# Delta stage on 32x32 tiles in token order, chunks of 64 tokens, filter products moved into the scan

## The reference

```python
q, k, v = short_conv(x @ Wq), short_conv(x @ Wk), short_conv(x @ Wv)   # 4 heads of 32
beta = sigmoid(x @ Wb); q, k = l2norm(q), l2norm(k); v = v * beta; kb = k * beta
A = -tril(kb @ k.T, -1)                       # per chunk of 32 tokens
T = solve_triangular(eye - A, eye, lower=True)
u = T @ v; w = T @ kb
def step(S, (qi, ki, ui, wi)):                # scan over the chunks
    attn = tril(qi @ ki.T)
    u_i = ui - wi @ S
    o_i = qi @ S + attn @ u_i
    return S + ki.T @ u_i, o_i
branches = [fir(v, fir_s), fir(v, fir_l), delta_o, v]   # filters of 3 and 31 taps
o = sum(gate(x, branches) * branches) ... @ Wo
```

## Time and profile before

| what | us |
|---|---|
| median of 3 runs | 594.73 |
| lowest, highest | 591.89, 598.05 |
| profiled execution, its time | 600.54 |
| its span in the trace | 598.8 |
| PE / PEld busy | 439.1 / 333.1 |
| DVE / ACT / POOL busy | 322.3 / 225.3 / 142.4 |

### The profile page before, as it was taken

The page is one execution under the profiler, slowest core; times in us unless marked ns, Lnnn a source line. Parts: engine busy times, 40 slices in busy tenths (PEclk is TensorE's granted clock), DMA queues, the critical chain, the costliest instruction groups (busy, mean ns, idle before and its releaser), DMA issues. The chain is left out here.

```text
span 598.8 us, 12845 instructions
## 1 busy us (share of the span) xinstructions
PE 439.1 (73%) x5009; PEld 333.1 (56%) x5010; DVE 322.3 (54%) x819; ACT 225.3 (38%) x453; POOL 142.4 (24%) x154
## 2 busy tenths in 40 slices
PE   0782699926976588899999999995999344029990
PEld 0682399913545467677875655563355344029890
DVE  4540355436965697776444654327368884216533
ACT  1232045514565278884231000017457222005550
POOL 4336025520006980000000000002023200733441
PEclk9999889966897679999679965558799655559996
DMA  9963301130000000000000000005400036140015
GB/s 174 261 199 88 101 15 37 35 89 1 0 1 0 4 4 4 5 4 3 1 2 1 2 0 1 0 1 123 106 1 1 0 120 197 44 128 24 32 35 155
DMA packets 32710, 29.93 MB, mean 50 GB/s; under 512 B 6800, under 2 KB 25776, under 8 KB 32656
## 3 DMA queue, kind: packets, MB, share of 16 engines
q1 hardware_dynamic: 23760, 20.96, 12.6%
q10 hardware_dynamic: 6400, 3.08, 3.4%
q0 software_dynamic: 2496, 5.13, 2.6%
HBM read 16.54 MB, written 9.21 MB: 43 GB/s over the span
## 5 line engine op out<-in xcount | busy, mean ns | idle before, releaser
L303 ACT ACTIVATE hT<-bank,b1s 128x128 f32<-128x128 f32 x184 | 52.4, 370 | 90.8 <-PE bank L260 90.6
L206 POOL DMA_INDIRECT ysort<-Y,row x46 | 44.8, 974 | 78.7 <-DVE Y L382 72.6
L260 PE MATMUL bank<-xT,w1s 128*128 (+1 forms) x368 | 51.5, 285 | 2.8 <-DVE xT L405 2.8
L276 PE MATMUL bank<-W,hT 128*128 x368 | 50.8, 281 | 3.6 <-ACT hT L303 3.1
L260 PEld LDWEIGHTS bank<-xT,w1s 128*128 128x128 f32 x368 | 47.0, 200 | 4.1 <-DVE xT L405 3.6
L1386 POOL TENSOR_TENSOR m_DSQ<-DEL 128x512 f32<-128x512 f32 x4 | 4.1, 1041 | 187.8 <-POOLq L767 185.1
L276 PEld LDWEIGHTS bank<-W,hT 128*128 128x128 f32 x368 | 45.2, 193 | 6.0 <-issue 5.8
L1056 DVE TENSOR_TENSOR d_BD<-bank,quarter 128x2048 f32<-128x2048 f32 x16 | 36.6, 2289 | 14.2 <-PE bank L760 14.2
L199 POOL DMA_INDIRECT xsort<-xr,pos x32 | 31.4, 981 | 48.4 <-DVE pos L361 39.3
L901 PE MATMUL bank<-XN,K 32*128 32x128 f32 x128 | 40.2, 403 | 1.6 <-DVE XN L1092 1.6
L966 ACT ACTIVATE d_BD<-d_TP 32x512 f32<-32x512 f32 x64 | 40.6, 634 | 0.9
(11 more groups left out here) (297 smaller groups left out, 939.4 us busy)
## 6 DMA issues: line engine op xcount, KB each, us to landing
W<-in_L_ffn_w SPq DMA_DIRECT2D x2, 2048.0 KB, 13.4
xsort<-pad ACTq DMA_DIRECT2D x2, 1483.5 KB, 23.1
xs<-xsort SPq DMA_DIRECT2D x10, 258.0 KB, 4.3
G<-ysort SPq DMA_DIRECT2D x8, 256.0 KB, 3.8
b2bc<-in_L_ffn_b SPq DMA_DIRECT2D x2, 512.0 KB, 20.3
m_pairs<-FS SPq DMA_DIRECT2D x4, 256.0 KB, 5.0
m_pairs<-firT SPq DMA_DIRECT2D x4, 256.0 KB, 4.9
m_pairs<-VP SPq DMA_DIRECT2D x4, 256.0 KB, 5.1
```

The costliest lines, as they stand in the source:

```text
L206: gp.indirect_dma_start(ysort, bass.IndirectOffsetOnAxis(row[:, t:t + 1], 0), Y[:, t, :], None).then_inc(y_stored, 16)
L260: mm = pe.matmul(pH[s % 2][:, j * P:(j + 1) * P], w1s[:, s, j * P:(j + 1) * P], xT[:, bass.ds(t, 1), :], start=True, stop=True)
L276: mm = pe.matmul(pY[s % 2][:, 0:D], hT[:, s % 2, j, :], W2[:, bass.ds(e, 1), j, :], start=(j == 0), stop=(j == FC - 1))
L303: act.activation(hT[:, s % 2, j, :], pH[s % 2][:, j * P:(j + 1) * P], ACT.Gelu, bias=b1s[:, s, j:j + 1]).then_inc(h_ready, 1)
```

## The change

Only `attn_delta` changes in what it computes, and in `attn_consts` the masks that it needs.

- The blocks of A and T are kept as `[P, head, tile, 32]` with the chunk on the partitions. Nothing is block-diagonal any more. A takes 256 products of 32x32x32, and 128 more (`a10`) give the off-diagonal blocks of the 64-token chunks.
- The inverse takes 16 steps, four levels by four heads. A step is `first` and `second`, each 64 products of 32x32x32; DVE masks 128x512 (instead of 128x2048), adds 128x512 and transposes on DVE. The PE transposes and ACT's copies are gone.
- `off_first` and `off_second` (32 products each, once per head) make the off-diagonal blocks of the 64-token inverse `T64`, with 16 copies by ACT, 8 by POOL and 8 by DVE.
- Scores: 128 products of 32 rows by 64 by 64. T @ v and T @ kb: 128 products each, on 64-row tiles, with results already in the layout that the scan reads.
- Scan: 16 steps of 64 tokens. `intra` moves into it (four matmuls per step and sequence). The 512 matmuls of `long_fir` move from the inverse into the first eight steps, 64 a step; `turn_fl` moves to steps 10 to 15, three transposes a step.
- `make_masks` gets three more selects of 128x128 on POOL in place of one, and `finish` five more reductions on DVE.

```diff
+    C, W = 32, 64
...
+    STEPS = NL * NH
+    STEPS_S = L // W
...
+    CH = 2 * P // STEPS_S
...
+AT = sb("AT", [P, NH, NT, C])
+TN = sb("TN", [P, NH, NT, C])
+TT = sb("TT", [P, NH, NT, C])
+PM = sb("PM", [P, 2, NT, C])
+OX = sb("OX", [P, NH, NT, C])
+T64 = sb("T64", [P, NH, NT, W])
...
+    for n in range(NT):
+        for c in range(CT):
+            for h in range(NH):
+                mm = pe.matmul(banks[h][quad(c), n * C:(n + 1) * C], KT[quad(h), tokens(n, c)], KBT[quad(h), tokens(n, c)],
+                               start=True, stop=True)
+    mm.then_inc(at_psum, 1)
+    for n in range(NT):
+        for p in range(HT):
+            for h in range(NH):
+                mm = pe.matmul(banks[4 + h][quad(2 * p), n * C:(n + 1) * C], KT[quad(h), tokens(n, 2 * p)],
+                               KBT[quad(h), tokens(n, 2 * p + 1)], start=True, stop=True)
+    mm.then_inc(a10_psum, 1)
+    pe.wait_ge(a10_ready, NH)
+    def first(s):
+        h = s % NH
+        pe.wait_ge(t_ready, s + 1)
+        if s >= 2:
+            pe.wait_ge(p1_ready, s - 1)
+        for n in range(NT):
+            for c in range(CT):
+                mm = pe.matmul(banks[4 + s % 2][quad(c), n * C:(n + 1) * C], AT[quad(c), h, n, :], TN[quad(c), h, n, :],
+                               start=True, stop=True)
+        mm.then_inc(p1_psum, 1)
+    def second(s):
+        h = s % NH
+        pe.wait_ge(p1_ready, s + 1)
+        if s >= 2:
+            pe.wait_ge(t_ready, NH + s - 1)
+        for n in range(NT):
+            for c in range(CT):
+                mm = pe.matmul(banks[6 + s % 2][quad(c), n * C:(n + 1) * C], PM[quad(c), s % 2, n, :], TT[quad(c), h, n, :],
+                               start=True, stop=True)
+        mm.then_inc(dt_psum, 1)
+    for s in range(STEPS):
+        first(s)
+        if s > 0:
+            second(s - 1)
+    second(STEPS - 1)
+    def scores(r):
+        if r == 0:
+            pe.wait_ge(at_ready, NH)
+        else:
+            pe.wait_ge(m_ready, NH)
+        for n in range(r * TH, (r + 1) * TH):
+            for p in range(HT):
+                for h in range(NH):
+                    mm = pe.matmul(banks[h][wide(p), n % TH * W:(n % TH + 1) * W], KT[quad(h), chunk(n, p)],
+                                   QT[quad(h), chunk(n, p)], start=True, stop=True)
+        mm.then_inc(m_psum, 1)
+    def off_first(h):
+        pe.wait_ge(t_ready, STEPS + h + 1)
+        if h >= 2:
+            pe.wait_ge(x_ready, h - 1)
+        for n in range(NT):
+            for p in range(HT):
+                mm = pe.matmul(banks[4 + h % 2][quad(2 * p + 1), n * C:(n + 1) * C], OX[quad(2 * p), h, n, :],
+                               TN[quad(2 * p), h, n, :], start=True, stop=True)
+        mm.then_inc(x_psum, 1)
+    def off_second(h):
+        pe.wait_ge(x_ready, h + 1)
+        if h < 2:
+            pe.wait_ge(t_ready, NH + STEPS)
+        else:
+            pe.wait_ge(t10_ready, h - 1)
+        for n in range(NT):
+            for p in range(HT):
+                mm = pe.matmul(banks[6 + h % 2][quad(2 * p), n * C:(n + 1) * C], OX[quad(2 * p + 1), h, n, :],
+                               TT[quad(2 * p + 1), h, n, :], start=True, stop=True)
+        mm.then_inc(t10_psum, 1)
+    off_first(0)
+    off_first(1)
+    scores(0)
+    off_second(0)
+    off_first(2)
+    off_second(1)
+    off_first(3)
+    off_second(2)
+    scores(1)
+    off_second(3)
+    pe.wait_ge(t10_ready, NH)
+    pe.wait_ge(even_ready, HT * NH)
+    pe.wait_ge(odd_ready, NH)
+    pe.wait_ge(m_ready, 2 * NH)
     for g in range(NG):
...
+        for n in range(g * TB, (g + 1) * TB):
+            for h in range(NH):
+                for p in range(HT):
+                    o = n % TB * P + h * DK
+                    mm = pe.matmul(banks[g][wide(p), o:o + DK], T64[wide(p), h, n, :], VB[wide(p), n, quad(h)], start=True, stop=True)
+        mm.then_inc(u0_psum, 1)
+        for n in range(g * TB, (g + 1) * TB):
+            for h in range(NH):
+                for p in range(HT):
+                    mm = pe.matmul(banks[4 + 2 * p + n // TH][quad(h), n % TH * W:(n % TH + 1) * W], KB[wide(p), n, quad(h)],
+                                   T64[wide(p), h, n, :], start=True, stop=True)
+        mm.then_inc(wt_psum, 1)
     pe.wait_ge(u0_ready, NG)
...
     pe.wait_ge(wt_ready, NG)
...
+    def intra(b, n):
+        p, tile = n % HT, b * TH + n // HT
+        for h in range(NH):
+            mm = pe.matmul(o_place(tile)[wide(p), quad(h)], M[h][wide(p), tile, :], U[wide(p), tile, quad(h)], start=False, stop=True,
+                           skip_group_check=True)
+        if p == HT - 1 and tile % TB == TB - 1:
+            mm.then_inc(o_psum, 1)
+    def long_fir(i):
+        j = i * CH // 2 // CB
+        if i * CH // 2 % CB == 0 and j >= 2:
+            pe.wait_ge(fir_taken, j - 1)
+        for c in range(i * CH // 2, (i + 1) * CH // 2):
+            for g in range(CT):
+                src = DEL if g % 2 == 0 else V
+                mm = pe.matmul(banks[5 + j % 2 * 2][quad(g), c % CB * NT:(c % CB + 1) * NT], FIRT[wide(g // 2), c, :],
+                               src[wide(g // 2), :, c], start=True, stop=True)
+        if (i + 1) * CH // 2 % CB == 0:
+            mm.then_inc(fir_psum, 1)
     def turn_fl(n):
         g, t = n // TB, n % TB
...
+        if t == 0:
+            pe.wait_ge(*((o_taken, g + 1) if g < 2 else (fl_taken, g - 1)))
+        tr = pe.transpose(banks[4 + g % 2 * 2][:, t * P:(t + 1) * P], FLt[:, n, :], cst["ident"][:])
         if t == TB - 1:
             tr.then_inc(fl_psum, 1)
+    HALF = STEPS_S // 2
     for n in range(STEPS_S):
         w_state(0, n)
         if n > 0:
             add_state(1, n - 1)
...
+            intra(1, n - 1)
+        if n == HALF:
+            pe.wait_ge(fir_taken, P // CB)
         q_state(0, n)
+        if n < HALF:
+            long_fir(2 * n)
         add_state(0, n)
+        intra(0, n)
         w_state(1, n)
         q_state(1, n)
...
+        if n < HALF:
+            long_fir(2 * n + 1)
+        elif n > HALF + 1:
+            for t in range((n - HALF - 2) * 3, min((n - HALF - 1) * 3, NT)):
+                turn_fl(t)
     add_state(1, STEPS_S - 1)
...
+    intra(1, STEPS_S - 1)
...
+    act.wait_ge(at_psum, 1)
+    for h in range(NH):
+        act.activation(AT[:, h, :, :], blocks(banks[h]), ACT.Copy, scale=-1.0).then_inc(at_ready, 1)
+    act.wait_ge(a10_psum, 1)
+    for h in range(NH):
+        for p in range(HT):
+            cp = act.activation(OX[quad(2 * p), h, :, :], blocks(banks[4 + h])[quad(2 * p), :, :], ACT.Copy, scale=-1.0)
+        cp.then_inc(a10_ready, 1)
+    act.wait_ge(t64_zero, 1)
+    def take_x(h):
+        act.wait_ge(x_psum, h + 1)
+        for p in range(HT):
+            cp = act.activation(OX[quad(2 * p + 1), h, :, :], blocks(banks[4 + h % 2])[quad(2 * p + 1), :, :], ACT.Copy)
+        cp.then_inc(x_ready, 1)
...
+    take_x(0)
+    take_x(1)
+    take_t10(0)
+    take_x(2)
+    take_t10(1)
+    take_x(3)
+    take_t10(2)
+    take_t10(3)
...
+    def take_o(k, bank):
+        act.wait_ge(o_psum, k + 1)
+        act.activation(DEL[:, (bank - 4) * TB:(bank - 3) * TB, :], banks[bank][:].rearrange("p (t c) -> p t c", c=P),
+                       ACT.Copy).then_inc(o_taken, 1)
...
+    gp.memset(T64[:].rearrange("p h n i -> p (h n i)"), 0.0).then_inc(t64_zero, 1)
...
+    gp.wait_ge(t64_zero, 1)
+    gp.wait_ge(short_fir, n)
+    for h in range(NH):
+        gp.wait_ge(t_ready, STEPS + h + 1)
+        for p in range(HT):
+            if h + p > 0:
+                gp.wait_ge(even_ready, HT * h + p)
+            gp.tensor_copy(T64[quad(2 * p), h, :, 0:C], TT[quad(2 * p), h, :, :]).then_inc(even_ready, 1)
...
+    for h in range(NH):
+        ve.wait_ge(at_ready, h + 1)
+        ch.step(ve.tensor_tensor(TT[:, h, :, :], AT[:, h, :, :], stacked(cst["t2mask"][:]), ALU.mult))
+        ch.step(ve.tensor_tensor(TT[:, h, :, :], TT[:, h, :, :], stacked(cst["istack"][:]), ALU.add))
+        ve.transpose(TN[:, h, :, :].rearrange("p n c -> p (n c)"), TT[:, h, :, :].rearrange("p n c -> p (n c)")).then_inc(t_ready, 1)
+    def add(s):
+        h = s % NH
+        ve.wait_ge(dt_psum, s + 1)
+        ch.step(ve.tensor_tensor(TT[:, h, :, :], TT[:, h, :, :], blocks(banks[6 + s % 2]), ALU.add))
+        ve.transpose(TN[:, h, :, :].rearrange("p n c -> p (n c)"), TT[:, h, :, :].rearrange("p n c -> p (n c)")).then_inc(t_ready, 1)
+    for s in range(STEPS):
+        ve.wait_ge(p1_psum, s + 1)
+        if s >= 2:
+            ve.wait_ge(dt_psum, s - 1)
+        ve.tensor_tensor(PM[:, s % 2, :, :], blocks(banks[4 + s % 2]), stacked(cst["qmask"][:, s // NH, :]), ALU.mult).then_inc(p1_ready, 1)
+        if s > 0:
+            add(s - 1)
+    add(STEPS - 1)
+    def odd(h):
+        ve.wait_ge(t64_zero, 1)
+        ve.wait_ge(t_ready, STEPS + h + 1)
+        for p in range(HT):
+            cp = ve.tensor_copy(T64[quad(2 * p + 1), h, :, C:W], TT[quad(2 * p + 1), h, :, :])
```

(51 more changed lines are left out.)

291 lines of the change are left out of this document (71 added, 220 removed).

## The result

Before 594.8 us (median of four runs), after 677.5 us (676.3 to 684.3, four): ratio 1.141, 95% interval 1.132 to 1.149. The change costs 83 us, where the forecast had +45.3.

The account below looks back on a forecast made before the run. PE's instruction supply, some 3.7 us per 256, was taken as the bound. Terms +12.4, +45.8, +7.5 and -20.4 gave +45.3 us: 645.8 from the profiled 600.54, as median 640, range 612 to 672.

Parts of the forecast that it names:

- What bounds the kernel: PE in `attn_delta` waits for its instructions: 256 take about 3.7 us to come, an fp32 matmul costs four.
- the signs that I named: Expected in the changed profile: inverse load bursts 3.7 us apart, over 30 instruction packets, DVE and ACT busy under a third.
- A, `a10`, OX: First stage up to `first(0)`: two more instruction blocks and eight ACT copies, ending at 220.6 against 208.2, +12.4 us.
- The DVE start: DVE's two sums and a transpose per head before the inverse, done at about 225; nothing charged.
- Inverse: 16 steps of 512 instructions, bound by supply: 30.8 blocks at 3.7 us, 114 us against 68.2, +45.8 us.
- Apply: Off-diagonals, scores, T @ v and T @ kb after the inverse: 42.5 against 35.0 us, +7.5 us.
- The upper bound, which was meant for 0.50: T @ v and T @ kb in the apply: 27.5 us at half clock, where 17.5 was taken.
- Scan: 16 steps at mixed clock, 75 us taken between 67.4 and 101; with the last copy 76.3 against 96.7, -20.4 us.
- my own bound for 0.50: Scan wholly at clock 0.50: steps of 7.1 us with the filter and 5.0 without, in all 101 us.
- The third rival: Clock stays at 0.50 from inverse to scan end: +26 us scan, +10 T @ v and T @ kb, 676 us; chance 0.15.

Follow-up runs that it names:

- the lone edit on the instruction count: Changed kernel with half the products in each inverse step, each of 64 instead of 32 moving columns: inverse 59.5 us, whole 618.7 us.
- the doubled work: Changed kernel with as many inverse products, each with 64 moving columns instead of 32: inverse 113.5 us, whole 674.6 us.
- the loop: Changed kernel with 64-column inverse products, 56 of 64 per half step issued by a two-turn engine loop: inverse 77.8 us, whole 636.0 us.
- the lifted scan: Changed kernel with 16 dummy products of 128x128 weights and 512 columns ahead of the scan: scan 101.1 us, whole 682.0 us.
- `intra` apart: Changed kernel, filter block and 16 dummy products ahead of the scan, `intra` in blocks before step 8 and at the end: scan 68.1 us, whole 675.4 us.
- `v_stats` late: Kernel before with DVE's four `v_stats` moved from the scan to behind its last `state`: 576.2 us, ratio 0.971.

## Why the prediction was wrong, step by step

- *What bounds the kernel*: right. The 3.7 us per 256 instructions read from a stage of 12.6 us carried a stage of 114; the lone edit on the instruction count (59.5 against 113.0 us), the doubled work (113.5) and the loop (77.8) show it. Of the signs that I named one was missed, and narrowly: DVE was busy for 34% of the inverse and not for under a third.
- *A, `a10`, OX*: right, `first(0)` after 24.4 us for 25.0. The DVE start that I had weighed is there: the sum takes 2.72 us for three heads under POOL's filter, as in the earlier trace rows, and 0.69 for the fourth. It is done at 229.4, 30.2 us into the part, where 29.4 was expected. `second(0)` waits 1.4 us for the mask behind it, which costs nothing: the next block of instructions comes at 230.8, 3.7 us behind the last.
- *Inverse*: right, 114.3 for 114. The tail of DVE and ACT lies in it.
- *Apply*: right in sum, 43.0 for 42.5. Its parts: 23.0 us for the off-diagonals and scores (23.6 expected) and 20.0 for T @ v, T @ kb and the last copies, where 18.9 was taken (17.5 between 14.8 and 27.5, and 1.4). That stage is at 0.50 with PE busy for 18.7 us of it. The upper bound, which was meant for 0.50, was too high by some 9 us.
- *Scan*: the term that failed. I took 75 us between 67.4 and 101; it was 109.7 (111.0 less 1.3 for the last copy), over the upper bound. Its steps at 1.00 were right (4.76 and 3.31 us measured against 4.86 and 3.13). What was wrong is the sentence that there is more PE work around the pauses, from which I took a clock of mostly 1.00. That `v_stats` and its pauses cost the clock is shown for the kernel before; in the changed scan, lifted to 1.00, it falls without a pause, while `intra` and the filter run, and unlifted it stands at 0.50 from the first step to the last. Of the 34.7 us, 26 are the way from 75 to my own bound for 0.50. The other 9 are two sizes at 0.50: the filter steps are 7.77 us (62.15 / 8) instead of 7.1, which makes 5.4, and the transposes 1.44 us for three, 7.7 in all where my bound had 4.2. The step without the filter was right, 5.09 for 5.0.
- *The third rival* named the right clock with a chance of 0.15 and a time of 676 us, which is near the 677.5 measured, but partly by luck: it had 10 us for the apply that did not come, and lacked the 9 of the scan. Its one reason, that a low clock does not recover, holds and is not the whole cause: lifted, the scan lost the clock by itself. With the two levels known from the earlier trace rows, a scan half at 1.00 and half at 0.50 before, the chance was too small.
- *What would have made it right*: one row was there to be seen. In the earlier trace rows the apply before, with PE busy for 94% of it, stands at 0.76. A busy PE was no guarantee of the clock, and I read it past.

## What to carry to other kernels

Count PE's instructions, four for an fp32 product, before cutting one large product into many small ones: in a straight stream this chip fed 256 in 3.3 to 3.7 us at either clock, so 4096 of them cost 53.5 us here however idle the other engines were. Then look at the granted clock of each stage, not only at PE's busy share, and try whether taking a pause away, or even one full product added to a step, gives the clock back: here the first was worth 2.9% of the kernel for four moved calls, and the second 40 us (616.6 to 576.9) where the filter's narrow products had been put into the steps of the scan. Judge an edit by the clock that it leaves to the stages behind it too.

## What the runs showed of the hardware

- PE's clock stood at 0.50 with PE busy for 99% of 111 us (by the profile, in which the ends of matmuls are modelled). The Trainium skill ("TensorE: Matmul & The Clock Gate", Part 1) has it follow how busy PE has been lately; by the busy share of the profile this trace does not agree. In the runs here it fell without any idle time in steps with products of 16 and 32 columns (at 401.0 us, in the lifted scan) and in a block of products of 32 (at 437.4, with `intra` apart). In the inverse, with PE busy for about half of the time, it stood at 1.00 with 64 columns in a product (15.9 of 30 us) and at 0.50 with 32 (62.5 of 114.3). Which quantity the chip looks at these runs don't settle.
- A clock once lost was not regained by steps that keep it: the 32-token steps ran 81 us at 0.50 behind the filter, and 68 us at 1.00 with `v_stats` late and the filter left in the inverse.
- A pause of PE did not always go with a fall: 0.78 us in the scan before was followed by one, 0.75 us in the scan with `intra` apart was not.
- A loop of PE's over 112 instructions turned back in 0.18 us and fed PE faster than a straight stream (77.8 against 113.5 us for as many products).
